# First FFN unit's products started on two of three normed token tiles, and reordered GNN queues, in a one-core transformer block

## What is computed

```
xn = layernorm(x)
x  = x + gnn(xn, edges) + mix(xn)          # gnn ends in  out @ wo.T + bo
y  = layernorm(x)
q, k, v = fff_q(y), fff_k(y), fff_v(y)
x  = x + softmax(q @ k.T / 32) @ v
# fff: 4 levels of decisions (15 node scores per token) choose one of 16 leaves;
#   hidden = relu(y @ w1[leaf] + b1[leaf]); out = hidden @ w2[leaf] + b2[leaf]
```

## Time and profile before

| | us |
|---|---|
| median of 3 runs | 782.43 |
| profiled execution | 780.38 |
| its span | 778.6 |
| TensorE busy | 749.6 (96%) |
| VectorE busy | 489.0 (63%) |
| ScalarE busy | 382.5 (49%) |
| Pool busy | 172.1 (22%) |

### The profile page before, as it was taken

How to read it: one execution, slowest core, us unless ns; L and a number is a source line. 1 busy time by engine, 2 the same in 40 slices (tenths; PEclk the granted TensorE clock), 3 DMA queues, 4 the chain that set the end, 5 groups by cost and what they waited for, 6 DMA issues and landing times.

```text
span 778.6 us, 12119 instructions
## 1 busy us (share of the span) xinstructions
PE 749.6 (96%) x4738; PEld 720.0 (92%) x4738; DVE 489.0 (63%) x935; ACT 382.5 (49%) x658; POOL 172.1 (22%) x139
## 2 busy tenths in 40 slices
PE   4998999999999999999999999997999999999998
PEld 3988999999999999999999999887999999999997
DVE  6878756774884777567676776656544554451542
ACT  5444655665564556576767554134343334431430
POOL 4724322312322220260312665200000000000000
PEclk9999999999999999999999999999999999999999
DMA  5511223123313331212131613321433233231302
GB/s 198 193 55 59 105 109 109 58 107 109 104 59 109 108 120 74 109 54 109 55 109 54 244 55 129 109 109 55 140 124 115 109 128 143 108 109 55 109 2 81
DMA packets 14389, 79.59 MB, mean 102 GB/s; under 512 B 3216, under 2 KB 3504, under 8 KB 5616
## 3 DMA queue, kind: packets, MB, share of 16 engines
q1 hardware_dynamic: 11088, 74.45, 26.3%
q0 software_dynamic: 2960, 4.26, 1.7%
q10 hardware_dynamic: 288, 0.14, 0.1%
HBM read 76.66 MB, written 2.19 MB: 101 GB/s over the span
## 4 chain that ended last, share of the span: by engine, by line
PE 81%; DVE 10%; ACT 6%; issue 2%; DMA 0%; DVEq 0%; ACTq 0%
PE g_bank L1412 45%; PE g_bank L1439 14%; PE o_bank L1495 4%; PE t_bank L1484 3%; DVE w_lo L862 2%; PE s_bank L1782 2%; PE s_bank L1472 2%; PE s_bank L1473 2%; ACT w_hi L493 2%; PE s_bank L1366 2%; PE g_bank L1366 2%; ACT q_st L530 1%; PE t_bank L1782 1%; ACT q_st L528 1%; DVE act_lo L950 1%
## 5 line engine op out<-in xcount | busy, mean ns | idle before, releaser
L1412 PE MATMUL g_bank<-act_hi,w_hi 128*128 128x384 f32 x632 | 220.1, 348 | 0.8 <-DVE k_st L904 0.8
L1412 PE MATMUL g_bank<-act_hi,w_lo 128*128 128x384 f32 x632 | 211.9, 335 | 0.0
L1412 PE MATMUL g_bank<-act_lo,w_hi 128*128 128x384 f32 x632 | 211.5, 335 | 0.0
L862 DVE TENSOR_TENSOR w_lo<-raw,w_hi 128x2048 fp32r<-128x2048 f32 x59 | 138.5, 2348 | 34.1 <-ACT w_hi L493 33.4
L493 ACT ACTIVATE w_hi<-raw 128x2048 fp32r<-128x2048 f32 x67 | 127.9, 1909 | 25.0 <-PE s_bank L1782 12.5
L1412 PEld LDWEIGHTS g_bank<-act_hi,w_hi 128*128 128x128 f32 x632 | 119.1, 188 | 3.8 <-issue 3.7
L1412 PEld LDWEIGHTS g_bank<-act_lo,w_hi 128*128 128x128 f32 x632 | 119.0, 188 | 0.0
L1412 PEld LDWEIGHTS g_bank<-act_hi,w_lo 128*128 128x128 f32 x632 | 118.6, 188 | 0.0
L416 POOL DMA_INDIRECT edge_table<-ew,eidx x51 | 63.4, 1244 | 151.1 <-DMA edge_table<-ew,eidx 148.3
L1004 DVE TENSOR_TENSOR pT_lo<-t_bank,pT_hi 128x384 fp32r<-128x384 f32 x96 | 50.5, 552 | 26.1 <-ACT pT_hi L594 25.5
L365 POOL TENSOR_TENSOR w_lo<-raw,w_hi 128x2048 fp32r<-128x2048 f32 x9 | 42.3, 4700 | 101.3 <-ACT w_hi L493 101.3
(11 more groups left out here) (258 smaller groups left out, 1546.5 us busy)
## 6 DMA issues: line engine op xcount, KB each, us to landing
raw<-wstream_dram SPq DMA_DIRECT2D x68, 1024.0 KB, 4.8
x_sb<-x_dram SPq DMA_DIRECT2D x3, 512.0 KB, 4.7
y_acc<-x_dram POOLq DMA_DIRECT2D x3, 512.0 KB, 5.7
out_dram<-out_sb SPq DMA_DIRECT2D x6, 256.0 KB, 2.0
edge_table<-ew,eidx POOLq DMA_INDIRECT x51, 2.2
edge_table<-mask POOLq DMA_DIRECT2D x1, 576.0 KB, 3.5
mask<-edge_table POOLq DMA_DIRECT2D x1, 576.0 KB, 4.2
bo_b<-bo_dram POOLq DMA_DIRECT2D x1, 512.0 KB, 7.2
```

Source lines behind the costliest of these rows:

```text
L862: V.tensor_tensor(flat(w_lo[s][:, :, :]), raw[:, s, :], flat(w_hi[s][:, :, :]), ALU.subtract) \
L1412: last = mm(out, w2[a], x2[b], start=k == 0 and a + b == 0, stop=not after and k == KT - 1 and a == 1)
```

## The change

**FFN.** Half m = 0 and m = 1 of unit U_FFN are accumulated in `t_bank[0]` and `t_bank[1]`. The high x high products run in two pieces, on the 256 columns of token tiles 0 and 1 (`early`) and on the 128 columns of tile 2 (`late`), between the node scores; the other two products follow over all 384 columns, with `node_tiles` between them. `leaf_tiles` comes behind all products of the unit, and its two leaf masks go into unit U_FFN + 1 after product 6. The transposes of token tile 2 go to `g_bank`, and those of token tile 0 are issued one `wo_tile` earlier. ScalarE's order is root 1, take 0, scaled 1 instead of root 1, scaled 1, take 0; the splits of U_FFN + 1 come before the node scores are taken, on both engines. In the first FFN pass the loops of `first_linear` are written out.

**GNN queues.** The second half of Q of the first group is taken after `split_hi/lo(U_GNN + 3)` and, on ScalarE, between the second and third exponential. In each group with a next one, both engines take the third transpose of head 1 before the next group's first half of Q. `inverse` becomes a reciprocal of 6 values and a copy of 384 columns. Pool waits for VectorE's low part of U_OUT + 2 before `split_gnn(2)` and for that of U_OUT + 4 before the last low part of `split_gnn(3)`.

```diff
-        ln_bank = [g_bank, s_bank[1:3], t_bank]
+        ln_bank = [[g_bank, s_bank[1:3], t_bank], [g_bank, s_bank[1:3], g_bank]]
...  Pool, split_gnn
+                if gi == GROUPS - 1:
+                    pool.wait_ge(w_lo_ready, lo_turn(U_OUT + 4) + 1)
                 nc.gpsimd.tensor_tensor(oTg_lo[:, both, :], o_acc[:, both, :], oTg_hi[:, both, :], ALU.subtract) \
...
             split_gnn(1)
+            pool.wait_ge(w_lo_ready, lo_turn(U_OUT + 2) + 1)
             split_gnn(2)
...  ScalarE (take_Q of the last mix group: the same line on VectorE)
-                        else:
+                        elif m == 0:
                             take_Q(n + 4, m, C_BIQ)
...
-            exps("gnn", Index(0), 0)
...
                     split_hi(n + 1)
+                    exps("gnn", g, 0, (0, 1))
+                    take_Q(n + -1, 1, C_BIQ)
+                    exps("gnn", g, 0, (2,))
...
                 split_hi(n + 2)
+                take_pT(tile(1), (2,))
                 if more:
                     take_Q(n + 1, 0, C_BIQ + 2 * (gi + 1))
-                take_pT(tile(1), (2,))
                 exps("gnn", g, 2)
...
-            norm(x1, 1, 1)
+            root(1, 1)
             take_norm(late, 0)
+            scaled(x1, 1, 1)
             split_hi(Index(U_FFN))
             take_norm(late, 1)
             norm(x1, 1, 2)
             take_norm(late, 2)
+            split_hi(Index(U_FFN + 1))
...  VectorE
-                V.reciprocal(rinv[:, :, :, :].rearrange("p t a d -> p a t d"),
-                             esum.rearrange("p (a t) -> p a t", t=NT)[:, :, :, None].to_broadcast([P, 2, NT, DH])) \
+                own.done(V.reciprocal(rsum, esum))
+                V.tensor_copy(rinv[:, :, :, :].rearrange("p t a d -> p a t d"),
+                              rsum.rearrange("p (a t) -> p a t", t=NT)[:, :, :, None].to_broadcast([P, 2, NT, DH])) \
...
                     split_lo(n + 1)
+                    take_Q(n + -1, 1, C_BIQ)
...
                 take_pT(tile(1), (2,))
+                if more:
+                    take_Q(n + 1, 0, C_BIQ + 2 * (gi + 1))
                 maxima("gnn", g, 2, (2,))
...
+            split_lo(Index(U_FFN + 1))
             dve.wait_ge(o_full, PV_NODE + 2)
...  TensorE
+            def first_part(m, w, x, cols, start=False):
+                for k in range(KT):
+                    mm(t_bank[m][:, cols], w[0][:, k, m * P:(m + 1) * P], x[:, k, cols], start=start and k == 0,
+                       stop=False)
...
+            wo_tile(1, 0, 2, between=in_half(0)).then_inc(wo_full, 1)
+            wo_tile(1, 1, 2).then_inc(wo_full, 1)
             norm_T(1, ln_fill, 1)
...
             node_scores(slice(0, P), False)
+            pe.wait_ge(w_hi_ready, U_FFN + 1)
+            pe.wait_ge(g_hi, ln_fill + 4 - 2 * GROUPS)
+            for m in range(2):
+                first_part(m, w0_hi, act_hi, early, start=True)
+            norm_T(1, ln_fill, 2)
             pe.wait_ge(g_free, ln_fill + 4 + 2)
             node_scores(slice(P, 2 * P), False)
-            norm_T(1, ln_fill, 2)
+            pe.wait_ge(g_hi, ln_fill + 6 - 2 * GROUPS)
+            for m in range(2):
+                first_part(m, w0_hi, act_hi, late)
             pe.wait_ge(g_free, ln_fill + 6 + 2)
             node_scores(slice(2 * P, N), True)
-
+            unit_ready(Index(U_FFN))
+            for m in range(2):
+                first_part(m, w0_hi, act_lo, slice(0, N))
+                if m == 0:
+                    node_tiles()
+                first_part(m, w0_lo, act_hi, slice(0, N))
...
+                    def first_masks(m, k):
+
+                        if (m, k) == (0, 1):
+                            for i in range(2):
+                                leaf_mask(i, t_bank[i][:, 0:N], u=0).then_inc(g_full, 1)
+
+                    if (f, u) == (0, 0):
+                        leaf_tiles()
+                        continue
+                    if (f, u) == (0, 1):
+                        gemm_T(n, act_hi, act_lo, after=leaf_mask, between=first_masks, free=fill_of(n).value())
```

More of the change, by code:

```diff
@@ L493, in split_hi, with take_T @@
                 nc.scalar.activation(flat(w_hi[s][:, :, :]), raw[:, s, :], ACT.Copy).then_inc(w_hi_ready, 1)
-            def take_T(n, hi, tile, bias, func=ACT.Identity, tiles=(0, 1)):
+            def take_T(n, hi, tile, bias, func=ACT.Identity, tiles=(0, 1), banks=g_bank):
                 for m in tiles:
@@ L810, in _ @@
             for f in range(3):
-                with act.Fori(0, 2) as it:
+                if f == 0:
+                    for u in range(2):
+                        first_linear(f, Index(U_FFN + u), Index(2 * u), t_bank if u == 0 else g_bank)
+                with act.Fori(0 if f else 1, 2) as it:
                     for s in range(2):
@@ L1194, in _ @@
                 maxima("gnn", g, 2, (0, 1))
-                if more:
-                    take_Q(n + 1, 0, C_BIQ + 2 * (gi + 1))
-                else:
+                if not more:
                     dve.wait_ge(resid_in, 16 * (NT + 2))
@@ L1281, in _, with first_linear @@
             last.then_inc(sel_ready, 1)
-            def first_linear(f, n, tile):
-                split_lo(n + 1)
+            def first_linear(f, n, tile, banks=g_bank):
+                if banks is g_bank:
+                    split_lo(n + 1)
                 for m in range(2):
@@ L1287, in first_linear @@
                     dve.wait_ge(g_free, (fill_of(n) + m).value(1, 2))
-                    own.done(V.tensor_scalar(h_tmp[:, :], g_bank[m][:, 0:N],
+                    own.done(V.tensor_scalar(h_tmp[:, :], banks[m][:, 0:N],
                                              pp[:, bass.ds((tile + (C_B1 + KT * f + m)).value(), 1)], 0.0,
@@ L1309, in _ @@
                  .then_inc(nsel_ready, 1)
-                with dve.Fori(0, 2) as it:
-                    own.begin(it, 4)
-                    for s in range(2):
-                        first_linear(f, Index(U_FFN + 8 * f + s, it, 2), Index(2 * s, it, 4))
-                    own.end(2)
+                if f == 0:
+                    for u in range(4):
+                        first_linear(f, Index(U_FFN + u), Index(2 * u), t_bank if u == 0 else g_bank)
+                else:
+                    with dve.Fori(0, 2) as it:
+                        own.begin(it, 4)
+                        for s in range(2):
+                            first_linear(f, Index(U_FFN + 8 * f + s, it, 2), Index(2 * s, it, 4))
+                        own.end(2)
                 if f == 2:
@@ L1377, in taken, with gemm_T @@
                 pe.wait_ge(g_free, f.value(1, 2))
-            def gemm_T(n, src_hi, src_lo, k0=0, tiles=(0, 1), after=None, halfway=None, at_start=None,
-                       at_end=None, between=None, hi_first=False):
+            def gemm_T(n, src_hi, src_lo, k0=0, tiles=(0, 1), after=None, halfway=None, at_end=None,
+                       between=None, hi_first=False, free=None):
                 s = n.slot(2)
@@ L1388, in gemm_T @@
                         unit_ready(n)
-                    pe.wait_ge(g_free, LN_FILLS - 4 + 2 if m == 0 and hi_first else f.value(1, 1))
+                    pe.wait_ge(g_free, LN_FILLS - 4 + 2 if m == 0 and hi_first else free or f.value(1, 1))
                     out, c = g_bank[m][:, 0:N], slice(m * P, (m + 1) * P)
@@ L1457, in norm_T @@
                     for k in range(4 * j, 4 * j + 4):
-                        last = nc.tensor.transpose(ln_bank[t][j][:, k % 4 * P:(k % 4 + 1) * P],
+                        last = nc.tensor.transpose(ln_bank[n][t][j][:, k % 4 * P:(k % 4 + 1) * P],
                                                    nat[:, t, k * P:(k + 1) * P], ident[:, :])
@@ L1767, in node_scores, with node_tiles @@
                     last.then_inc(o_full, 1)
+            def node_tiles():
+                pe.wait_ge(o_free, PV_NODE + 2)
+                for t in range(NT):
+                    last = nc.tensor.transpose(o_bank[:, t * 48:(t + 1) * 48], h_tmp[0:48, t * P:(t + 1) * P],
+                                               ident[0:48, 0:48])
+                last.then_inc(o_full, 1)
+            def first_part(m, w, x, cols, start=False):
+                for k in range(KT):
+                    mm(t_bank[m][:, cols], w[0][:, k, m * P:(m + 1) * P], x[:, k, cols], start=start and k == 0,
+                       stop=False)
             def wo_tile(c, kh, t, between=None):
@@ L1798, in _, with in_half, norm_at @@
             wo_tile(1, 1, 1).then_inc(wo_full, 1)
-            wo_tile(1, 0, 2).then_inc(wo_full, 1)
-            def first_norm(k):
-                if k == 0:
-                    norm_T(1, ln_fill, 0)
-            wo_tile(1, 1, 2, between=first_norm).then_inc(wo_full, 1)
+            def in_half(t):
+                def norm_at(k):
+                    if k == 2:
+                        norm_T(1, ln_fill, t)
+                return norm_at
+            wo_tile(1, 0, 2, between=in_half(0)).then_inc(wo_full, 1)
```

(6 more changed lines are left out.)

29 lines of the change are left out of this document (11 added, 18 removed).

## The result

The kernel after takes 771.50 us (median of 4 executions, 771.42 to 771.92) where the kernel before takes 782.25 (median of 4, 780.17 to 783.72): ratio 0.9867, 95% interval 0.9851 to 0.9882, faster by 10.7 us. Forecast were 773.8 us and a range of 772.3 to 776.6: the sign is right and each part of the sum gave about what was forecast for it, but the time lies 0.8 us under the range, and that comes from something that was not in the sum. The profiled execution goes from 780.38 to 771.42 us, by 8.96, where the sum of the parts said 8.6.

A forecast was written before the change was run, and what follows sets the result against it. TensorE was taken as the bound, with its waiting before 560 us winnable: 1.7 + 2.5 + 0.7 + 3.7 = 8.6 us, taking the median from 782.43 to 773.8 us; range 772.3 to 776.6.

The forecast's parts named there:

- the last one of the sum: Whole kernel: profiled 780.38 goes to 771.8; lying 2.05 under the median, the median goes from 782.43 to 773.8 us.
- Rival D: Denser TensorE work between 527 and 560 lowers its clock, making the kernel slower: 793.8 us; chance 0.02.
- Start of the GNN heads: First group: ScalarE's high part and VectorE's split come before Q's second half, removing T(0, 2)'s wait; gain 1.7 us.
- Third transpose before Q: Three GNN groups: taking the third transpose first removes the second output product's wait; gain 2.5 us.
- Rival A: GNN groups: Q's later half step makes T(2, 1) or the row minima late; costs 2.5, 776.3 us; chance 0.12.
- Inverse: GNN heads: the 2.55 us `inverse` becomes short reciprocal and copy; nobody's releaser in the waits, gain 0.
- Pool's two new waits: GNN heads: Pool going second ends TensorE's `y_acc` wait, gain 0.7 us; the wait before `split_gnn(2)` brings 0.
- Second LayerNorm: Waits before scores 1, scores 2 and mask removed, 5.0 us, less new wait and split-product costs; gain 3.7 us.
- The new wait before transposes 2: Second LayerNorm: TensorE waits for tile 2's scaled row before its transposes; costs 0.45 us.
- The late products: Second LayerNorm: 16 products of 128 columns with full 128-column weights, pitch 0.10 us, between 0.068 and 0.120.
- Rival B: Second LayerNorm: late products take 0.174 each or the mask waits again; stage gives 2.2, 775.3 us; chance 0.07.
- Rival C: Second LayerNorm: the first FFN unit isn't started early, its inputs coming after 529.3; costs 3.7, 777.5 us; chance 0.03.

The follow-up runs named there:

- e3: Kernel before with only the GNN queue changes of ScalarE, VectorE and Pool: 775.57 us, ratio 0.9928.
- e4: Kernel before plus 16 useless 256-column products in TensorE's first idle stretch of the second LayerNorm, before scores 1: 780.92 us, ratio 0.9988.
- e5: Kernel before with VectorE's split of U_FFN ahead of the low parts scores 1 wait for, lengthening that wait: 784.95 us, ratio 1.0042.
- e9: Kernel before with only the third transpose of head 1 taken before the next group's first half of Q, on both engines: 779.62 us, ratio 0.9970.
- e11: Kernel before plus 16 useless 256-column products in the second idle stretch, before scores 2, the first left unfilled: 781.31 us, ratio 0.9993.
- e1: Kernel after run again without edit, beside the kernel before: 771.82 us, ratio 0.9871.
- e8: Kernel after with the single slow 384-column reciprocal put back in `inverse`: 772.16 us, ratio 0.9876 to the kernel before.
- e6: Kernel after with Pool's U_OUT + 2 wait moved before the low part of `split_gnn(1)`, and a wait added in `split_gnn(0)`: 770.71 us.
- e2: Kernel before with only the second LayerNorm and first FFN unit part of the change: 777.40 us, ratio 0.9945.
- e7: Kernel after with each 128-column late product done as two of 64 columns: 774.48 us, ratio 0.9912 to the kernel before.
- e12: The same kernel as e10 run again on another chip: 774.46 us, ratio 0.9902 to the kernel before.
- e10: Kernel after with U_FFN's high x high products in one piece of 384 columns behind the scores of tile 2: 773.56 us, ratio 0.9897 to before.

## Why the prediction was right or wrong, point by point

**The step that failed is the last one of the sum:** "it lies 2.05 under the median, so the median goes from 782.43 to 773.8". It carries the profiled execution's distance from the median over to the new kernel as if it were a constant. It isn't one. Some 1.5 us of it (782.43 against 780.9, the median at full clock) are executions in which the clock falls to 1.2 GHz in the second LayerNorm, and the change fills just that stretch: in after all eight executions are at 1.00, and the median of the first four lies 0.1 over their profiled one. The other 0.5 is luck of one execution: in the profiled one of before TensorE's first product starts at 8.77 us, in the traces of e3, e4, e5, e9 and e11, which share this start, at 9.29 to 9.51. That of after has it at 8.91, the one of e1 at 9.52. With the 0.36 by which the sum was short this is the whole miss: 1.5 + 0.5 - 0.1 + 0.36 = 2.3 = 773.8 - 771.5. A sum made against the profiled execution alone gave 771.8. The parts measured below come to 9.1; the profiled executions differ by 8.96, since that of after began 0.14 later.

**Rival D had the clock with the wrong sign.** It asked whether denser work lowers the clock. It is idle time that does: e4 adds work and loses no clock in 12 executions, e5 adds idle time and loses it in all seven. The Trainium skill's page "TensorE: Matmul & The Clock Gate" (What's actually happening; HAM oscillation) says that the slow clock is the default and activity releases it, and that idle gaps in TensorE's work bring it back. It speaks of longer gaps than the 2.15 us here, so it would not have called this one; there the measurement decides. By a rule of its kind the change would give the clock back on top of the waits. It was a rival with a price that could have been worked out (behind the first idle stretch of the earlier trace rows stand 48 node products and eight transposes, 2 x 1.5 + 0.8 = 3.8 us of work, which half speed doubles, less the 1.57 us of idle time among them: up to 2.2 us), and it wasn't weighed. The spread of the three times of before (782.07 to 783.72, all over the profiled 780.38) was the sign of it.

**Start of the GNN heads**, forecast 1.7, measured 1.77. The new split ended at 320.92 (317.16 + 3.76) where 320.9 was forecast, and V's second half wasn't held.

**Third transpose before Q**, forecast 2.5 for three, measured 2.96 (0.97, 0.97 and 0.99 at the three products, the rest between them). The mechanism is right and stands alone (e9), the size of one term is not: 0.16 was added to each wait for the modelled end. Before, after the wait, reads

```profile
338.49 0.44 PE L1495 MATMUL o_bank<-pT_hi,v_st 128*128 128x384 f32 x1 [0.69 <-DVE pT_lo L1004]
338.77 0.34 PE L1495 MATMUL o_bank<-pT_lo,v_st 128*128 128x384 f32 x1
338.94 0.34 PE L1495 MATMUL o_bank<-pT_hi,v_st 128*128 128x384 f32 x1
```

and the first product behind a wait takes 0.28 us to the next instead of 0.17. So a wait of 0.7 costs 0.95 to 1.0, not 0.85. Rival A (Q late for T(2, 1)) did not happen: the wait for `o_acc` is 0.2 us in all in after, as it was before. A small hand-on of the kind, 0.35 at T(2, 2) of the first group, shows in e9 and is kept out of after by the new `inverse`.

**Inverse**, forecast 0, measured 0.34 in the traces (e8). The step was "it is nobody's releaser in the waits": true of before, where T(2, 2) waited 0.09, and no longer true with the third transpose ahead of Q. Without it the change would gain 0.34 less.

**Pool's two new waits**, forecast 0.7, measured 0.83; the one before `split_gnn(2)` 0, as forecast, and e6 shows what it would have been worth in its right place: 0.69, and 1.11 together with the one in `split_gnn(0)`.

**Second LayerNorm**, forecast 3.7, measured 3.53 (e2 3.5). The new wait before transposes 2 is 0.21 + 0.16 = 0.37, forecast 0.45. The late products have a pitch of 0.112, forecast 0.10 within 0.068 to 0.120, which costs 0.2. The forecast's own working for the 0.10, 1.04 less 0.27 over 7, gives 0.11, and with that the stage comes to 3.55. Rival B (0.174 each) did not happen, and e7 shows why: the 128-column weights and not the columns are what is paid. Its price was off too: with 1.9 in place of 0.74 the stage gives 2.5, not 2.2. Rival C did not happen: the early products began at 523.81 without a wait.

**The range** came from the sum's bounds and rivals A and B, all on the slow side; nothing on the fast side was in it but cheap late products. The miss was there.

**What stays open**: what decides in a given execution whether the clock falls. Executions of the same kernel with the same waits do either, and e12 differs from e10 in nothing but the chip and the moment. Open too is where the clock fell in e7, and why the slow reciprocal is felt in the first group alone.

## What to carry to other kernels

Before the sum of a profiled execution is carried over to a median, ask why the two differ: list the mean clock of every execution, and if there are steps in it, look for the idle stretch of TensorE that is ahead of the fall, because filling it can pay twice, as it did here. A term put at nothing because nobody waits for it in the trace of before holds only as long as the other edits leave its neighbours where they are. A price for a removed wait is its length plus the refilling behind it (0.2 to 0.3 us here). And a wait that is to stop two engines from colliding has to stand before the instruction that collides, which the trace names.

## What the runs showed of the hardware

- TensorE's clock fell to 1.2 GHz in 35 of 61 executions of before. It cost 1.4 us (mean clock 0.998) or 2.4 (0.996). Where a trace has the fall, it comes behind an idle stretch of 2.15 to 2.17 us that follows 24 node products (e9, e11, e12) or at the end of one of 4.35 us (e5). 16 products with no use in that stretch removed it in 12 of 12 executions (e4).
- It also fell in 2 of 4 executions of a kernel that waits at most 0.21 us in the second LayerNorm and runs 32 products of 64 columns there (e7); the place of the fall isn't traced.
- Products with 128-column weights cost 0.112 us with 128 as with 64 columns (after, e7), and products of 128 columns with 48-column weights 0.06.
- Two-input VectorE and Pool instructions over SBUF ran one after the other: 3.71 to 3.88 us instead of 2.28 for the one that came second, and nothing for the first: Pool's part took 1.83 to 1.85 when it ran first and 1.84 when it ran alone (e6).
- The first product behind a wait of 0.69 us took 0.28 us to the next instead of 0.17, and a removed wait of that length gave 0.97 to 0.99 (e9).
